# The tail of a layer-norm, recurrence and expert kernel: bias rows made one tile sooner, first states between two down products, last columns in pieces

## The reference

```python
xn = layernorm(x)                                  # over the last axis of 256
A = sigmoid(log_A)
B_x = einsum('btd,nd->btn', xn, B_w) + B_b
h = scan(h_t = A * h_{t-1} + B_x_t)                # 256 states, over time
s = einsum('btn,dn->btd', h, C_w) + C_b
logits = xn @ Wr + br                              # 8 experts, the best two of each token
y = sum over the two of weight * ((silu(xn @ W1[e]) * (xn @ W3[e])) @ W2[e])
g = silu(y)
out = x + s * g
```

## Time and profile before

| | us |
|---|---|
| median of 3 runs | 835.05 (834.76 to 836.0) |
| the profiled execution, whole | 835.19 |
| its span in the trace | 833.4 |
| PE busy in the span | 799.0 (96%) |
| DVE, POOL, ACT busy | 508.1, 438.8, 372.8 |

### The profile page before, as it was taken

How to read it: one execution, slowest core, us unless ns; L and a number is a source line. 1 busy time by engine, 2 the same in 40 slices (tenths; PEclk the granted TensorE clock), 3 DMA queues, 4 the chain that set the end, 5 groups by cost and what they waited for, 6 DMA issues and landing times.

```text
span 833.4 us, 17056 instructions
## 1 busy us (share of the span) xinstructions
PE 799.0 (96%) x5608; PEld 717.6 (86%) x5608; DVE 508.1 (61%) x1079; ACT 372.8 (45%) x658; POOL 438.8 (53%) x345
## 2 busy tenths in 40 slices
PE   2999979999999999999999999999999999998996
PEld 2554448999999999999999999999999999997885
DVE  6878954565766665666656554555564654552665
ACT  3884143444545444445445444445454544442520
POOL 4632241665665765666765666666666656634000
PEclk9999999999999999999999999999999999999999
DMA  9979731333544433334434433434453433423994
GB/s 296 348 250 319 117 97 44 58 64 57 131 65 107 83 64 55 58 65 104 85 67 103 84 65 53 60 65 102 85 117 76 71 68 51 62 39 39 314 341 152
DMA packets 88190, 93.35 MB, mean 112 GB/s; under 512 B 15266, under 2 KB 79524, under 8 KB 88164
## 3 DMA queue, kind: packets, MB, share of 16 engines
q0 software_dynamic: 27264, 37.39, 28.0%
q1 hardware_dynamic: 51460, 55.32, 20.7%
q10 hardware_dynamic: 9440, 0.34, 0.9%
HBM read 48.66 MB, written 44.37 MB: 112 GB/s over the span
## 4 chain that ended last, share of the span: by engine, by line
PE 90%; DVE 7%; DMA 1%; issue 1%; ACT 0%; POOL 0%; DVEq 0%
PE bank L1129 16%; PE bank L1128 16%; PE bank L1130 16%; PE bank L1158 16%; PE bank L1159 8%; PE bank L1205 7%; PE bank L1117 4%; PE bank L1030 3%; DVE xnT L797 2%; PE bank L994 2%; DVE stats L666 1%; PE bank L1201 1%; PE bank L1006 1%; DVE xnT L809 1%; DMA x_sb<-L_attn_x 1%
## 5 line engine op out<-in xcount | busy, mean ns | idle before, releaser
L424 POOL DMA_INDIRECT y_rows<-y_sb,token_idx x142 | 230.5, 1623 | 217.0 <-DVE y_sb L875 175.1
L1128 PE MATMUL bank<-xh,W_sb 128*128 128x256 f32 x1136 | 318.9, 281 | 3.1 <-issue 1.6
L1129 PE MATMUL bank<-xh,W_sb 128*128 128x256 f32 x1136 | 319.4, 281 | 0.0
L1130 PE MATMUL bank<-xl,W_sb 128*128 128x256 f32 x1136 | 318.5, 280 | 0.0
L863 DVE TENSOR_TENSOR hbuf<-hbuf,bank 128x512 f32<-128x512 f32 x142 | 97.6, 687 | 217.7 <-PE bank L1130 216.4
L1128 PEld LDWEIGHTS bank<-xh,W_sb 128*128 128x128 f32 x1136 | 215.0, 189 | 6.7 <-issue 3.5
L1129 PEld LDWEIGHTS bank<-xh,W_sb 128*128 128x128 f32 x1136 | 214.7, 189 | 0.0
L1130 PEld LDWEIGHTS bank<-xl,W_sb 128*128 128x128 f32 x1136 | 213.8, 188 | 0.0
L1158 PE MATMUL bank<-W_sb,hh 128*128 128x512 f32 x568 | 209.3, 407 | 1.1 <-DVE y_sb L875 1.1
L415 POOL DMA_INDIRECT xg<-xn_rows,token_idx x142 | 165.6, 1166 | 67.4 <-issue 43.0
L1159 PE MATMUL bank<-W_sb,hl 128*128 128x256 f32 x568 | 159.6, 281 | 0.0
(11 more groups left out here) (156 smaller groups left out, 638.5 us busy)
## 6 DMA issues: line engine op xcount, KB each, us to landing
raw<-L_ffn_W SPq DMA_DIRECT2D x24, 512.0 KB
x_sb<-L_attn_x SPq DMA_DIRECT2D x16, 512.0 KB, 6.7
xn_rows<-h_sb SPq DMA_DIRECT2D x16, 512.0 KB, 5.0
y_rows<-xnT SPq DMA_DIRECT2D x4, 2048.0 KB, 16.8
yy<-y_rows SPq DMA_DIRECT2D x16, 512.0 KB, 8.8
out<-x_sb SPq DMA_DIRECT2D x15, 512.0 KB, 7.5
xg<-xn_rows,token_idx POOLq DMA_INDIRECT x142
y_rows<-y_sb,token_idx POOLq DMA_INDIRECT x142
```

Of the source, the lines that this page charges most:

```text
L424: eng.indirect_dma_start(out=y_rows, out_offset=bass.IndirectOffsetOnAxis(ap=token_idx[:, 2 * i + t:2 * i + t + 1], axis=0), in_=y_sb[:, i ...
L1128: eng.matmul(part, high, x_h, start=k == 0, stop=False)
L1129: eng.matmul(part, low, x_h, start=False, stop=False)
L1130: last = eng.matmul(part, high, x_l, start=False, stop=k == KD - 1)
```

## The change

- The C loads wait for the low parts of W1 and W3 only; `Cb_raw` moves to where `Cb_hi` was, and `Cb_hi` is gone: the high part is written into row 32 of `Cb_rows` and the low parts are made from it in place.
- VectorE's clearing of `pick` and `Cb_rows` stands one expert step sooner (before `add_y(68)`), and its two subtractions stand before `add_y(69)`, no more after `add_y(70)`.
- `keep_C` on ScalarE stands before `keep_y_low(69)`, and `transpose_C` on TensorE before down(69).
- `states_out(0)` stands between down(69) and down(70); it also waits for the last `silu`, since it writes banks 0 and 1, which hold the last gate.
- VectorE's order in the tail: apply of a chunk's first half, addition of the second half of the chunk before, apply of the second half, addition of the first half.
- Chunk 15 is made, applied, added and stored in three pieces, of 512, 256 and 256 columns (`LAST_PARTS`), the third in bank 0.
- `y_ready` 71 is waited for before chunk 3, no more before chunk 2.

```diff
@@ -56,6 +56,7 @@
 LOWEST = -3.0e38
...
 CB_ROWS = (0, 32)
+LAST_PARTS = ((0, 2 * D, 5), (2 * D, D, 7), (3 * D, D, 0))
 S_BANKS = ((0, 1), (2, 3), (4, 6), (5, 7))
@@ -133,11 +134,10 @@
         with ExitStack() as tail:
...
             Cb_rows = sb("Cb_rows", [P, 2 * D], f32r, tail)
-            Cb_hi = sb("Cb_hi", [P, D], f32r, tail)
+            Cb_raw = sb("Cb_raw", [P, D], f32, tail)
             Cw_raw = sb("Cw_raw", [P, KD, N_STATE], f32, tail)
             CwT = sb("CwT", [P, KN * D], f32, tail)
-            Cb_raw = sb("Cb_raw", [P, D], f32, tail)
-            pad_to_weights = sb("pad_to_weights", [P, W_COLS - 2 * KN * D - 4 * D - P], f32, tail)
+            pad_to_weights = sb("pad_to_weights", [P, W_COLS - 2 * KN * D - 3 * D - P], f32, tail)
             yy = sb("yy", [P, CHUNKS, CT * D], f32, tail)
@@ -326,7 +326,7 @@
                     eng.dma_start(raw[:, at:at + cols].rearrange("p (k i) -> p k i", k=k), W_v[n][:, e, :, :]).then_inc(raw_loaded[n], 16)
-            for n in range(3):
+            for n in range(2):
                 eng.wait_ge(w_low[n], E)
@@ -340,11 +340,11 @@
             for c in range(CHUNKS - 1):
...
                 eng.dma_start(out_v[:, c * CT:(c + 1) * CT, :], x_sb[:, c * CT:(c + 1) * CT, :]).then_inc(out_stored, 16)
-            for n in range(2):
-                at = (CHUNKS - 1) * CT + n * CT // 2
+            for n, (at, cols, b) in enumerate(LAST_PARTS):
+                j = (CHUNKS - 1) * CT + at // D
                 eng.wait_ge(out_ready, 2 * CHUNKS - 1 + n)
-                eng.dma_start(out_v[:, at:at + CT // 2, :], x_sb[:, at:at + CT // 2, :]).then_inc(out_stored, 16)
-            eng.wait_ge(out_stored, 16 * (CHUNKS + 1))
+                eng.dma_start(out_v[:, j:j + cols // D, :], x_sb[:, j:j + cols // D, :]).then_inc(out_stored, 16)
+            eng.wait_ge(out_stored, 16 * (CHUNKS - 1 + len(LAST_PARTS)))
         @block.gpsimd
@@ -580,8 +580,8 @@
             def keep_C():
                 eng.wait_ge(c_loaded, 48)
-                eng.activation(Cb_hi[CB_ROWS[1]:CB_ROWS[1] + 1, :], Cb_raw[CB_ROWS[1]:CB_ROWS[1] + 1, :], ACT.Copy).then_inc(Cb_hi_ready, 1)
                 eng.wait_ge(rows_cleared, 1)
+                eng.activation(Cb_rows[CB_ROWS[1]:CB_ROWS[1] + 1, 0:D], Cb_raw[CB_ROWS[1]:CB_ROWS[1] + 1, :], ACT.Copy).then_inc(Cb_hi_ready, 1)
                 for n in range(2):
@@ -598,7 +598,6 @@
                     keep_y_low(i - 1)
...
                 if not gate:
-                    keep_C()
                     return
@@ -620,6 +619,7 @@
                     expert_step(i0 + n, (n + 1) % 2)
...
             expert_step(last - 1, 1, xT=False)
+            keep_C()
             expert_step(last, 0, gate=False, xT=False)
@@ -931,9 +931,6 @@
                     expert_step(i0 + n, n, i0 * 16 + (n - 1) // 2 * 32)
...
             expert_step(last - 2, 0, 16 * (last - 2) - 32)
-            expert_step(last - 1, 1, 16 * (last - 2), xT=False)
             eng.memset(pick[:, :].bitcast(f32), 0.0).then_inc(dve_step, 1)
@@ -941,37 +938,44 @@
             for row in CB_ROWS:
                 eng.memset(pick[row:row + 1, :].bitcast(f32), 1.0).then_inc(Cb_ready, 1)
+            expert_step(last - 1, 1, 16 * (last - 2), xT=False)
+            low_row = slice(CB_ROWS[1], CB_ROWS[1] + 1)
+            eng.wait_ge(Cb_hi_ready, 1)
+            link(eng.tensor_tensor(Cb_rows[low_row, D:2 * D], Cb_raw[low_row, :], Cb_rows[low_row, 0:D].bitcast(f32), ALU.subtract))
+            eng.tensor_tensor(Cb_rows[low_row, 0:D], Cb_raw[low_row, :], Cb_rows[low_row, 0:D].bitcast(f32), ALU.subtract).then_inc(Cb_ready, 1)
             expert_step(last, 0, 16 * (last - 2), gate=False, xT=False)
             add_y(last, 0, 16 * last)
-            low = slice(CB_ROWS[1], CB_ROWS[1] + 1)
-            eng.wait_ge(rows_cleared, 1)
-            eng.wait_ge(Cb_hi_ready, 1)
-            for n in range(2):
-                eng.tensor_tensor(Cb_rows[low, n * D:(n + 1) * D], Cb_raw[low, :], Cb_hi[low, :].bitcast(f32), ALU.subtract).then_inc(Cb_ready, 1)
-            def apply(c):
+            def apply(c, at, cols, b, done):
+                two = yy[:, c, at:at + cols]
+                eng.wait_ge(s_psum, done)
+                eng.tensor_tensor(two, two, bank[b][:, 0:cols], ALU.mult).then_inc(u_ready, 1)
+            def add_x(c, at, cols, done):
+                eng.wait_ge(u_ready, done)
+                x_g = x_sb[:, c * CT:(c + 1) * CT, :].rearrange("p t d -> p (t d)")[:, at:at + cols]
+                eng.tensor_tensor(x_g, yy[:, c, at:at + cols], x_g, ALU.add).then_inc(out_ready, 1)
+            for c in range(CHUNKS - 1):
                 eng.wait_ge(g_ready, c + 1)
-                for n, b in enumerate(S_BANKS[c % len(S_BANKS)]):
-                    two = yy[:, c, n * 512:(n + 1) * 512]
-                    eng.wait_ge(s_psum, 2 * c + n + 1)
-                    eng.tensor_tensor(two, two, bank[b][:, :], ALU.mult).then_inc(u_ready, 1)
-            def add_x(c, n):
-                eng.wait_ge(u_ready, 2 * c + n + 1)
-                x_g = x_sb[:, c * CT + n * CT // 2:c * CT + (n + 1) * CT // 2, :].rearrange("p t d -> p (t d)")
-                eng.tensor_tensor(x_g, yy[:, c, n * 512:(n + 1) * 512], x_g, ALU.add).then_inc(out_ready, 1)
-            for c in range(CHUNKS):
-                apply(c)
+                apply(c, 0, 512, S_BANKS[c % 4][0], 2 * c + 1)
                 if c:
-                    for n in range(2):
-                        add_x(c - 1, n)
-            for n in range(2):
-                add_x(CHUNKS - 1, n)
+                    add_x(c - 1, 512, 512, 2 * c)
+                apply(c, 512, 512, S_BANKS[c % 4][1], 2 * c + 2)
+                add_x(c, 0, 512, 2 * c + 1)
+            c = CHUNKS - 1
+            eng.wait_ge(g_ready, CHUNKS)
+            for n, (at, cols, b) in enumerate(LAST_PARTS):
+                apply(c, at, cols, b, 2 * c + 1 + n)
+                if n == 0:
+                    add_x(c - 1, 512, 512, 2 * c)
+                add_x(c, at, cols, 2 * c + 1 + n)
         @block.tensor
@@ -1184,30 +1188,33 @@
                     down(i, (n + 1) % 2)
...
             up(EXP_TILES - 1)
+            transpose_C()
             down(EXP_TILES - 2, 1)
-            transpose_C()
-            down(EXP_TILES - 1, 0, last=True)
+            def states_out(c):
+                h_g = h_half(c // 2 * 2, c % 2)
+                last_chunk = c == CHUNKS - 1
+                for n, (at, cols, b) in enumerate(LAST_PARTS if last_chunk else ((0, 2 * D, S_BANKS[c % 4][0]), (2 * D, 2 * D, S_BANKS[c % 4][1]))):
+                    if c >= len(S_BANKS):
+                        reused = CHUNKS - len(S_BANKS) if n == 2 else c - len(S_BANKS)
+                        eng.wait_ge(u_ready, 2 * reused + n % 2 + 1)
+                    eng.matmul(bank[b][:, 0:cols], pick[:, :], Cb_rows[:, 0:cols], start=True, stop=False)
+                    for t in range(at // D, (at + cols) // D):
+                        o = bank[b][:, t * D - at:(t + 1) * D - at]
+                        for m in range(KN):
+                            last = eng.matmul(o, h_g[:, m, t * P:(t + 1) * P], CwT[:, m * D:(m + 1) * D],
+                                              start=False, stop=(t + 1) * D == at + cols and m == KN - 1)
+                    last.then_inc(s_psum, 1)
             eng.wait_ge(scan_done, 4 * BATCH)
             eng.wait_ge(CwT_ready, 1)
-            eng.wait_ge(Cb_ready, 6)
-            def states_out(c):
-                h_g = h_half(c // 2 * 2, c % 2)
-                for n, b in enumerate(S_BANKS[c % len(S_BANKS)]):
-                    if c >= len(S_BANKS):
-                        eng.wait_ge(u_ready, 2 * (c - len(S_BANKS)) + n + 1)
-                    eng.matmul(bank[b][:, :], pick[:, :], Cb_rows[:, :], start=True, stop=False)
-                    for t in range(2 * n, 2 * n + 2):
-                        o = bank[b][:, (t % 2) * D:(t % 2 + 1) * D]
-                        for m in range(KN):
-                            last = eng.matmul(o, h_g[:, m, t * P:(t + 1) * P], CwT[:, m * D:(m + 1) * D],
-                                              start=False, stop=t % 2 == 1 and m == KN - 1)
-                    last.then_inc(s_psum, 1)
-            for c in range(CHUNKS):
-                if c == 2:
+            eng.wait_ge(Cb_ready, 5)
+            eng.wait_ge(silu_ready, 2 * EXP_TILES)
+            states_out(0)
+            down(EXP_TILES - 1, 0, last=True)
+            for c in range(1, CHUNKS):
+                if c == 3:
                     eng.wait_ge(y_ready, EXP_TILES)
```

## The result

The changed kernel takes 831.24 us (median of 7 runs, 829.69 to 832.12) against 835.05 us (7 runs, 833.54 to 836.0): a ratio of 0.9957, 95% interval 0.9947 to 0.9968, so 3.6 us less (2.7 to 4.4). The forecast was 3.7 us less and 831.35 us. The profiled execution took 830.82 us, its span is 829.0.

The account below looks back on a forecast made before the run. TensorE, 90% of the chain, was taken as the bound, with time only in its idle stretches and behind its last matmul. 1.40 (PE) + 1.44 (VectorE) + 0.86 (stores) = 3.7 us, 835.05 to 831.35 us; range 830.1 to 833.3.

Parts of the forecast that it names:

- Both gaps go: PE's idle stretches before down(70), 1.55 us, and before the first bias matmul, 2.33 us, would both disappear.
- The y chain decides chunk 4: From y_low and add_y through scatter(70), yy loads, silu and apply: PE stops 2.3 us before chunk 4, gaining 1.40 us.
- The end: Behind PE's last matmul: reordered additions with pieces bring VectorE's end 1.44 us closer, the stores give another 0.86 us.
- The 3.5 us beside the sum: Alternative total gain, with the last 128 KB store priced at 2.3 us from a skill page, beside the 3.7 us.
- rival D: The clock falls to half in the gap before chunk 4 for 6.6 us, costing 3.3 us: 834.65 us, no change; 5%.
- 12 us of steady work ahead of this one: Argument against a clock fall before chunk 4: steady PE work precedes this gap, unlike an earlier gap followed by a fall.
- Rivals A and B: Before chunk 4: A, the y chain passes its whole delay, 833.1 us, 7%; B, PE doesn't wait, 828.9 us, 3%.
- Rival C: Rows not ready for the states of chunk 0 at 757.31; 1.5 us late leaves 2.2 us gained, 832.85 us; 4%.

Follow-up runs that it names:

- changed again: The changed kernel without any edit, measured a second time: 831.25 us, ratio 0.9958 to the kernel before.
- order and pieces: The kernel before with only the new order of additions and chunk 15 in three pieces: 831.49 us, ratio 0.9968 to the kernel before.
- first load split: The changed kernel with the first load of yy and its silu in two parts of 512 columns: 828.32 us, ratio 0.9927 to the kernel before.
- rows late: The changed kernel with keep_C on ScalarE back behind keep_y_low of tile 69: 836.30 us, ratio 1.0014 to the kernel before.
- rows and states only: The changed kernel without the new order of additions and without the pieces: 833.99 us, ratio 0.9994 to the kernel before.
- nothing before down(70): The changed kernel with states of chunk 0 behind down(70) and transposes back between the two down products: 829.97 us, ratio 0.9946 to the kernel before.

## Why the prediction was right

The time, the direction and the mechanisms were right. That the 3.7 us were met to a hundredth is luck in part: PE's end comes 1.17 us sooner from the reference event (72.45 to 71.28; forecast 1.40), VectorE's last addition 1.51 us closer behind it (3.12 to 1.61; forecast 1.44), and the span's end 1.03 us closer behind that (3.69 to 2.66; forecast 0.86). The misses cancel. One attribution and the price of the clock were wrong.

- **Both gaps go.** Right. The start of the states is 0.09 us behind the end of down(69) where 0 was counted, and the first matmul there takes 0.47 where 0.23 was counted: 0.3 us. It passes one for one to down(70), whose y_low starts at 10.23 us from the event where 9.93 was forecast, and to scatter(70), 12.48 for 12.18. The profile names no wait for the 0.09 us ("issue"); the rows and CwT were ready before.
- **The y chain decides chunk 4.** Right, with the terms: POOL released 0.86 us after the addition, SP's loads 5.63 us after scatter(70), a stop of 2.03 us for 2.3. From the loads to the first apply it took 0.15 less than before. PE's gain at chunk 4's first half is 1.32 us (its end, 779.65, is 26.20 from the event; before 27.52), forecast 1.40. At chunk 15 it is 1.18, because in this one trace half chunks came every 1.960 us; in the traces of before, of "changed again", of "order and pieces" and of "first load split" they came every 1.953 or 1.954.
- **The end.** Right as a sum: 2.53 for 1.44 + 0.86 = 2.30. The prediction gives these for the order and the pieces together, and takes the second near its upper bound for two reasons, the backlog of 512 KB and the half size of the last piece. The half size was no reason: with the new order and no pieces VectorE gives 1.68 us and the stores 0.84, together 2.52. What is left for the stores is that chunk 14 is added, and so stored, sooner. The pieces shorten the last landing by 0.19 us and lengthen VectorE's end by 0.18.
- **The 3.5 us beside the sum.** They can't be followed from the prediction's own terms: a last store issued at 826.9 that takes 2.3 us lands at 829.2, which is 4.2 us sooner, not 3.5. The last store of 128 KB took 2.3 us in "first load split"; the median of the two small ones in the changed kernel is 2.5.
- **The clock, rival D.** Given 5%, and priced at 3.3 us from a stretch of 6.6 us. It is no rival but a part of the kernel: by the mean clock it was absent in the seven runs that were compared and present in three of six later ones, at 1.5 us. "12 us of steady work ahead of this one" was an argument, and no protection. That the forecast's seven runs had no fall was luck too.
- **Rivals A and B** are out: the landing of scatter(69) did hide part of the delay, since taking that delay away brought the first apply only as far as the landing allows (22.59, against 22.30 before plus 0.44 for the transposes), and PE did wait. Rival C didn't happen, since the rows were ready; "rows late" shows that it would have cost 2.5 us for its 2.6 us, and a fall of the clock besides.

Left open: what makes the clock fall after one gap and not after another. In the traces of this tail stops before chunk 4 of 2.24 and 2.16 us were followed by a fall and those of 2.03 and 2.08 us were not, but the gap of 2.35 us before the states in the kernel before was not either. Of that kernel's runs two of eleven in each of two groups and one of fifteen in a third have a mean clock of 0.992 too, and none of 22 in a fourth.

## What to carry to other kernels

When work is pulled ahead of the producer of a second chain, compare how long that chain is delayed with how long its consumer can wait. Here 3.9 us of states were put ahead of down(70), and the four chunks of buffers between the two chains hid only part of it. It was better to take the small serial steps off the path, to shorten the transfer that is waited for, and to leave the producer first. In a tail, look for work that could be done already and is queued behind work that can't: reordering additions gave 2.5 us. Cutting the last work into pieces showed no gain, because the engine was still busy with other work when the first piece became ready.

## What the runs showed of the hardware

- A load of 256 KB landed 2.70 us after its issue ("first load split"), one of 512 KB 4.00 (changed kernel), from the same DRAM buffer at the start of the same queue's burst: halving the first transfer of a burst saved 1.3 us. From issue to silu it was 2.7 to 2.8 us in the four traces with the split and 4.0 to 4.2 in those of before, of "order and pieces", of both of the changed kernel, of "rows and states only" and of "nothing before down(70)".
- Behind a single PE stop of 2.24 us in an otherwise full stretch the granted clock was still full when PE started again, fell to half about 1.3 us later and stayed there for 3.4 us, at a cost of 1.7 us ("rows and states only"). By the mean clock 11 of 11 runs of that kernel had such a fall, and 3 of 13 of the changed kernel, whose traced stops are 2.03 and 2.08 us and which differs only behind the stop.
- The granted clock as a mean over the span (0.995 or 0.993) sorts runs of one kernel into two groups 1.5 us apart, which the median alone hides.
- A matmul of 128x512 on the chain takes 0.47 to 0.50 us at full clock when it is the first after a stop, even one of 0.09 us, and 0.23 in the stream.
